# One program for the rotary projections and the attention loop, and a new order of the first expert group

## The reference, cut to what matters

```python
def _attn(x, ln_w, ln_b, conv_w, attn_w, proj_w, n_head):   # C = 256, n_head = 16, D = 16, T = 64
    h = _layernorm(x, ln_w, ln_b)
    hc = jax.lax.conv_general_dilated(pad(transpose(h)), conv_w, ...)     # 3 taps, per feature
    qkv = transpose(hc) @ attn_w
    q, k, v = jnp.split(qkv, 3, axis=-1)                                  # each (B, T, n_head, D)
    q = q * cos + _rotate_half(q) * sin
    k = k * cos + _rotate_half(k) * sin
    scores = jnp.einsum('bqhd,bkhd->bhqk', q, k) / jnp.sqrt(jnp.float32(D))
    p = jax.nn.softmax(jnp.where(causal, scores, -1e30), axis=-1)
    y = jnp.einsum('bhqk,bkhd->bqhd', p, v).reshape(B, T, C)
    return y @ proj_w
# x = x + _attn(...); then logits = layernorm(x) @ router_w, an argmax over four experts, and the chosen expert's FFN
```

## Time and profile before

| what | us |
|---|---|
| median of three runs | 2086.64 |
| lowest and highest run | 2083.78, 2087.58 |
| the profiled execution | 2082.32 |
| its span, first to last instruction | 2080.5 |
| TensorE busy | 1919.6 (92%) |
| VectorE busy | 1431.5 (69%) |
| ScalarE busy | 1103.8 (53%) |
| GpSimd busy | 848.8 (41%) |

### The profile page before, as it was taken

One profiled execution on the slowest core, in us unless ns is written; L12 is line 12 of the kernel. 1 busy time (PEld: TensorE's weight loads), 2 busy tenths in 40 slices (PEclk: granted clock), 3 DMA queues, 4 the chain that ended last, 5 costly groups with the idle time before them and its releaser, 6 DMA issues. The chain is left out here.

```text
span 2080.5 us, 35356 instructions
## 1 busy us (share of the span) xinstructions
PE 1919.6 (92%) x12240; PEld 1616.1 (78%) x12240; DVE 1431.5 (69%) x2403; ACT 1103.8 (53%) x2116; POOL 848.8 (41%) x855
## 2 busy tenths in 40 slices
PE   8999999999999999999998576999999666949998
PEld 6788888888888888888887455888899455839998
DVE  7767676767767676767776895432698565847776
ACT  5554555545555554555544697232455364636664
POOL 6350321405042240404200285130498144868885
PEclk9999999999999999999999699999999887969999
DMA  4101010010101010010102201310266114556661
GB/s 154 62 1 61 1 61 0 20 41 0 60 0 60 0 39 22 0 60 0 28 1 72 51 3 56 110 49 1 73 217 194 44 44 140 178 197 203 217 212 47
DMA packets 96322, 144.51 MB, mean 69 GB/s; under 512 B 15358, under 2 KB 72608, under 8 KB 96096
## 3 DMA queue, kind: packets, MB, share of 16 engines
q1 hardware_dynamic: 89168, 127.21, 19.0%
q0 software_dynamic: 4928, 12.86, 1.7%
q10 hardware_dynamic: 2128, 3.15, 0.4%
HBM read 111.46 MB, written 14.16 MB: 60 GB/s over the span
## 5 line engine op out<-in xcount | busy, mean ns | idle before, releaser
L317 PE MATMUL ps<-cond_x_lo,cond_w_hi 128*128 128x512 f32 x1008 | 393.4, 390 | 0.0
L468 ACT ACTIVATE cond_h_hi<-cond_h 128x512 fp32r<-128x512 f32 x288 | 174.0, 630 | 294.3 <-DVE cond_h L647 294.2
L781 POOL TENSOR_TENSOR cond_w_lo<-cond_stage_up,cond_w_hi 128x512 fp32r<-128x512 f32 x36 | 46.9, 1304 | 588.6 <-ACT cond_w_hi L468 588.6
L317 PE MATMUL ps<-cond_x_hi_first,cond_w_hi 128*128 128x512 f32 x578 | 230.8, 399 | 6.1 <-DVE cond_h L647 4.7
L378 PE MATMUL ps<-cond_h_hi,cond_d_hi 128*128 128x512 f32 x576 | 224.6, 390 | 2.6 <-DVE cond_h_lo L652 2.6
L317 PE MATMUL ps<-cond_x_hi_first,cond_w_lo 128*128 128x512 f32 x578 | 225.6, 390 | 0.0
L378 PE MATMUL ps<-cond_h_hi,cond_d_lo 128*128 128x512 f32 x576 | 224.2, 389 | 0.0
L378 PE MATMUL ps<-cond_h_lo,cond_d_hi 128*128 128x512 f32 x576 | 224.2, 389 | 0.0
L317 PEld LDWEIGHTS ps<-cond_x_lo,cond_w_hi 128*128 128x128 f32 x1008 | 189.9, 188 | 37.2
L630 DVE TENSOR_TENSOR ps<-cond_p_row,ps 128x512 f32<-128x512 f32 x142 | 98.6, 694 | 171.2 <-PE ps L317 171.1
L515 ACT ACTIVATE cond_h<-ps 128x512 f32<-128x512 f32 x216 | 124.6, 596 | 165.3 <-DVE cond_h_lo L652 132.1
(11 more groups left out here) (422 smaller groups left out, 5121.2 us busy)
## 6 DMA issues: line engine op xcount, KB each, us to landing
moe_stage_up<-in_L_ffn_expert_wv SPq DMA_DIRECT2D x22, 1024.0 KB, 9.2
typed_stage_up<-in_L_cond_wi SPq DMA_DIRECT2D x11, 1024.0 KB, 5.0
typed_stage_dn<-in_L_cond_wo SPq DMA_DIRECT2D x11, 1024.0 KB
moe_stage_dn<-in_L_ffn_expert_proj SPq DMA_DIRECT2D x11, 1024.0 KB
cond_stage_up<-in_L_cond_Wg SPq DMA_DIRECT2D x7, 1024.0 KB, 5.0
cond_stage_up<-in_L_cond_Wu SPq DMA_DIRECT2D x7, 1024.0 KB, 7.2
cond_stage_dn<-in_L_cond_Wd SPq DMA_DIRECT2D x7, 1024.0 KB, 9.4
rope_v_now<-rope_v_blk SPq DMA_DIRECT2D x16, 272.0 KB, 2.4
```

What stands on the lines that cost most here:

```text
L317: ins = pe.matmul(bank, ws[:, j, u, w], xs.rearrange("p o n -> p (o n)"), start=(opens and k == 0), stop=(k == 2), skip_group_check=True)
L468: copy = lambda dst, src: act.activation(dst, src, ACT.Copy)
L781: return pool.tensor_tensor(w_lo[:, j, :, A11:A12 + 1], raw_up[:, :, :, upper(j)], w_hi[:, j, :, A11:A12 + 1], ALU.subtract)
```

## The change

It has three parts. All three only move work or place it elsewhere in memory; what is computed is the same.

1. In the first stage, group 0: VectorE makes the hidden products as soon as their products are there, between the splits of T3 and T4; GpSimd splits T1 and T2 (new semaphore `x_lo_first`); ScalarE keeps both raw blocks of tokens (four copies instead of two). The split of the sums of chunk 0, which group 1 doesn't use, goes behind that of chunk 2, and `up_ready` is counted accordingly. ScalarE rounds hidden tiles of group 0 and then the weights of chunk 2 inside group 1.
2. `attention` becomes `hyper_attention` (the hyperbolic one, its lines unchanged) and `rotary`. The latter has one block: iterations 0 to 2 of the loop are written out between the projections 10 to 15, the loop's lists start at iteration 3 (EARLY). Projections use banks 4 to 7, since the loop's first phases use 0 to 3. The buffers u and prob lie where xT was, k_blk, x, qT and y in the space of s0, the projections' input, and pT in that of src_hi. So `bring(0)` waits for `src_ready` of all four wide tiles, `p_turn(0)` for the last `qk_taken` and `mix(0)` for the last `v_taken`. The router's weights are loaded at the beginning of the block. Four of the eight value copies follow in iterations 3 to 6, and the rotation of tile 15 in iteration 3.
3. At the end: VectorE does norm, weigh and lift of tile 15 (`finish`), GpSimd only its total. The logits of tiles 11 to 15 go to columns of their own in the bank (`late_ps`) and are copied together.

The diff, cut to its core:

```diff
@@ paired_experts
-                        pe.wait_ge(up_ready, J * e + j + 1)
+                        pe.wait_ge(up_ready, g if isinstance(g, int) and g <= 2 else J * e + j + 1)
...
+                def plain():                                   # VectorE
+                    plain_copy(0)
+                    hidden(0, 0, p2_done, bank_a, 0)
+                    split_t(T3)
+                    hidden(0, 0, p3_done, bank_d, 1)
+                    split_t(T4)
+                    plain_copy(1)
+                    dve.wait_ge(c22_made, 2)
+                    hidden(0, 0, c22_made, p5_row[:], 2)
+                    dve.wait_ge(x_lo_first, 2)
+                    dve.wait_ge(x_lo_dve, 6)
+                    split(0, 0, 12, 1)
+                    split(0, 0, 22, 2)
+                    hidden(0, 0, p4_done, bank_b[1], 3)
...
-                            plain_copy(0)
-                            for i in (T1, T2, T3, T4):
-                                split_t(i)
-                            dve.wait_ge(x_lo_dve, 8)
-                            dve.wait_ge(turned, 2 * TT)
-                            for t in range(2):
-                                keep_raw(1, t)
...
-                split_sums(0, 0)
-                split_sums(0, 1)
+                for n in range(2):                             # GpSimd
+                    pool.wait_ge(x_rounded, 2 * KC + n + 1)
+                    pool.tensor_tensor(x_lo[:, T1 + n:T1 + n + 1, cols(0)], t_first[:, n:n + 1], x_hi(T1 + n, 1, cols(0)),
+                                       ALU.subtract).then_inc(x_lo_first, 1)
+                split_sums(0, 1, 1)
                 split_down(0, 0)
+                raws(0, 2)
                 split_down(0, 1)
-                raws(0, 2)
-                split_sums(0, 2)
+                split_sums(0, 2, 2)
+                split_sums(0, 0, 3)
@@ rotary
+        u, prob = placed(m.xT_at, ("u", [2, H, T]), ("prob", [2, H, T]))
+        k_blk, x, qT, y = placed(src_at, ("k_blk", [2, KC, 2, GH, T]), ("x", [2, QK]), ("qT", [2, KC, P]), ("y", [2, D]))
+        pT, = placed(hi_at, ("pT", [2, HP, P]))
...
+                router.load(sp)                                # SyncE
+                double(0)
+                double(1)
+                sp.wait_ge(src_ready, TT)
+                bring(0, 0, 0)
+                bring(1, 1, 0)
+                double(2)
+                bring(2, 0, 1)
+                sp.wait_ge(ones_set, 1)
+                fetch(0, 0, 0)
+                double(3)
+                run(sp, "sync", ...)
...
+                for i in range(NP):                            # TensorE
+                    project(i)
+                    if i == 10:
+                        turn(0, 0, 0)
+                    elif i == 11:
+                        score(0, 0, 0)
+                    elif i == 12:
+                        turn(1, 1, 0)
+                    elif i == 14:
+                        score(1, 1, 0)
...
+                for i in range(NP):                            # ScalarE
+                    take_projections(i)
+                    if i == 3:
+                        round_src(2)
+                    elif i == 7:
+                        round_src(3)
+                        block_values(0, 0)
+                    elif i == 8:
+                        block_values(0, 1)
+                    elif i == 9:
+                        block_values(1, 0)
+                    elif i == 10:
+                        block_values(1, 1)
+                        take_q(0, 0, 0)
+                    elif i == 12:
+                        take_q(1, 1, 0)
+                    elif i == 14:
+                        exponential(0, 0, 0)
...
+                for i in range(NP):                            # VectorE
+                    times_cos(i)
+                    if i >= 1:
+                        rotate(i - 1)
+                    if i == 3:
+                        split_src(2)
+                    elif i == 7:
+                        split_src(3)
+                    elif i == 10:
+                        block_k(0, 0, 0)
+                    elif i == 12:
+                        clamp(0, 0, 0)
+                        top(0, 0, 0)
+                    elif i == 13:
+                        block_k(1, 1, 0)
...
+                for i in range(NP):                            # GpSimd
+                    times_sin(i)
+                    if i == 13:
+                        shift(0, 0, 0)
...
+                def finish(i, q, nth):                         # VectorE, in iteration i + 5, tile 15 alone
+                    dve.wait_ge(averaged, i + 1)
+                    dve.wait_ge(rstd_done, i + 1)
+                    dve.wait_ge(lifted, i - 1)
+                    dve.tensor_scalar(xn, router.x2[:, q], router.mean[:, q, 0:1], router.rstd[:, q:q + 1],
+                                      ALU.subtract, ALU.mult).then_inc(last_steps, 1)
+                    dve.wait_ge(last_steps, 1)
+                    dve.tensor_tensor(xn, xn, router.w[:], ALU.mult).then_inc(last_steps, 1)
+                    dve.wait_ge(last_steps, 2)
+                    dve.wait_ge(h_turned, i - 1)
+                    dve.wait_ge(stored[q], 16 * nth)
+                    dve.tensor_tensor(router.rows[:, q, 0:D], xn, router.b[:], ALU.add).then_inc(last_lifted, 1)
...
+                    wait(pe, kept, LATE if late(i) else i)     # route
+                    lg = late_ps[:, (i - LATE) * E_MOE:(i - LATE + 1) * E_MOE] if late(i) else lg_ps
```

More of the change, by code:

```diff
@@ L1 @@
+import math
 from contextlib import ExitStack
@@ L742, in expert @@
                             take(of_e, of_p, RIGHT if j == 0 else LEFT, first)
[L743 to L744 removed]
+                        combine(e, c, 1)
                         hidden(e, c, p2_done, bank_a, 0)
                         hidden(e, c, p3_done, bank_d, 1)
[L747 to L750 removed]
+                        lower_right(e, c, 1)
                         dve.wait_ge(c22_made, 2 * (CY * e + c) + 2)
@@ L1575, in hyper_units, with hyper_attention @@
     sem.give_back()
-def attention(nc, m, tag, hyper, srcT, resT, w, router=None, stored=None):
-    QK, GH = 2 * D, H // 4
+def hyper_attention(nc, m, tag, srcT, resT, w):
+    QK = 2 * D
     HP = H // 2
@@ L1660, in _ @@
                             n = 0
-                            more = hyper and cols.start == QK
+                            more = cols.start == QK
                             for k in range(KC):
@@ L1863, in _ @@
                             split_src(i // SUB + 2)
-                    later(NP - 1)
-                    if hyper:
-                        for part in range(6):
-                            norms(1, part)
-                        spikes()
+                    space_norm(NP - 1)
+                    for part in range(6):
+                        norms(1, part)
+                    spikes()
                 @block.gpsimd
@@ L1888, in _ @@
-                    if not hyper:
-                        for i in range(NP):
-                            times_sin(i)
-        sem.give_back()
-        if hyper:
-            hyper_units(nc, m, tag, resT, qk, v_blk, space, spike, wo, bo)
-            return
-        if hyper:
-            lag = dict(turn=0, q_blk=0, k_blk=0, score=0, clamp=1, root_sq=1, root_ln=2, root=2, root_add=2, dist_ln=2,
-                       dist=3, mask=3, top=3, shift=3, prob=4, p_turn=4, p_take=4, mix=5, y=5, y_turn=5, y_take=6,
-                       out=6, add=6, stretch=0, fetch=3)
-            order = dict(tensor="mix out turn p_turn y_turn score",
-                         scalar="y_take dist root_ln prob root q_blk root_sq p_take dist_ln",
-                         vector="stretch clamp y add k_blk top", gpsimd="mask root_add shift", sync="fetch")
-        else:
-            lag = dict(bring=0, turn=1, q_blk=1, k_blk=1, score=1, clamp=2, top=2, shift=2, prob=2, p_turn=3, p_take=3,
-                       mix=3, y=3, y_turn=4, y_take=4, out=4, fetch=2, bring_sum=3, bring_x=5, x2=4, stats=5, aggr=5, rstd=5,
-                       total=5, norm=5, weigh=5, lift=5, h_turn=8, h_take=8, route=9, keep=9, store=7)
-            order = dict(tensor="h_turn y_turn p_turn turn out mix route score",
-                         scalar="y_take h_take p_take rstd q_blk x2 prob",
-                         vector="stats clamp top aggr k_blk y keep", gpsimd="shift total norm weigh lift",
-                         sync="bring fetch bring_sum bring_x store")
@@ L1912, in attention @@
-        last = max(lag.values())
-        sem = StageSemaphores(nc, tag)
-        stretched, turned, k_turned, q_taken, k_blocked = (
-            sem(n) for n in ("stretched", "turned", "k_turned", "q_taken", "k_blocked"))
-        scored, clamped, root_squared, root_logged, rooted = (
-            sem(n) for n in ("scored", "clamped", "root_squared", "root_logged", "rooted"))
```

(3 more changed lines are left out.)

933 lines of the change are left out of this document (498 added, 435 removed).

## The result

| what | us |
|---|---|
| median before, beside it | 2085.72 (2083.78 to 2087.58) |
| median after | 2068.09 (2066.73 to 2071.58) |
| ratio | 0.9918, interval 0.9905 to 0.9930 |
| profiled execution, its span | 2071.58, 2069.8 (before: 2082.32, 2080.5) |
| measured again, beside the first experiments | 2070.38, ratio 0.9929 (0.9916 to 0.9943) |

What follows compares the result with a forecast made beforehand. The prediction took waits at the start, the join of rotary projections to attention loop, and the loop's end as the bounds; 3.5 + 14.5 + 2.4 = 20.4 us off the median 2086.64 gives 2066.2, range 2060.5 to 2076.

Steps and rivals of the forecast that it cites:

- Place 1, the start: First expert group: hidden products ahead of the T splits bring the first down product earlier; 3.5 us, bounds 1.5 and 5.5.
- what follows is as late relative to it as before: Start, behind the first down product: combine at 33.3, a wait of 0.8, so the 4.0 us lead is kept.
- Place 2, the join: Rotary projections to attention loop: the chain woven into the last projections gains 14.5 us, bounds 9 and 16.5.
- the brought tile's wait: Join, behind tile 10: TensorE waits 1.2 us, up to 2.4, for bring(0), with projection 11 and all others behind it.
- the wait for `k_blk(1)`: Join, score 1 behind projection 14: TensorE waits 1.8 us for VectorE's k_blk of tile 1, projection 15 behind it.
- covered: Join, tiles 7 to 10: ScalarE falls 1.2 us behind with four value copies; the banks and TensorE's wait absorb it.
- no wait for the brought tile, copies hidden: Join: the case behind the upper bound of its gain, 16.5 us.
- Place 3, the end: Loop's end: VectorE does norm, weigh and lift of tile 15, choose comes earlier; 2.4 us, bounds 1.5 and 3.5.
- The late bring: Rival at the join: bring lands 5 us late, score 1 as well; join gives 8, about 2073.5; chance 0.20.
- The clock falls at the join: Rival, TensorE's waits from 1728 to 1735: half clock lengthens the chain by 2.4 us, 2068.6; no chance of its own.
- The lead given back in the loop: Rival: the join's lead only makes tiles wait in the loop; places 1 and 3 remain, 5.9 us, 2080.7; chance 0.04.
- the stretch of the loop's operations by their place in memory: Rival: clamp, max and k_blk take 1.65 each instead of 1.2; 23 us over 17 iterations, 2089; chance 0.03.

Runs made afterwards that it cites:

- the first experiments: Before with the new start alone, 2081.88 us; before with the merged rotary block alone, 2074.62; after with the old end of the loop, 2073.66.
- the three kernels: After with value copies of tiles 4 to 7 moved later, 2071.62 us; with loads of x ahead of the second doubling, 2071.57; with both, 2066.37.
- the first kernels: Before with the merged rotary block alone, 2074.62 us; after with the old end of the loop, 2073.66 us.
- bring first: After with the loads of x of tiles 0 and 1 issued ahead of SyncE's second doubling: 2071.57 us, ratio 0.9937.

## Why the prediction was right, and where it wasn't
- **Place 1, the start: right in the first step, wrong in the second, and near the figure since two errors met.** The first product's wait fell from 4.68 to 0.23 us and is released by GpSimd's split of the sums, as said. The first down product started at 30.30 (29.5 to 30.0 in the other profiles; forecast 31.4), which is 1.1 to 1.9 better than forecast. The step that failed is "what follows is as late relative to it as before": it holds only if VectorE's operations keep their length, and they didn't, since the change also fills the 8 us in which GpSimd had been idle beside them. 5.1 became 2.4 here, and 5.5 to 5.9 became 2.7 to 3.6 in the others, against 3.5 forecast and bounds of 1.5 and 5.5. The postponed sum split, which the forecast guarded with 2 us, cost nothing that I could find.
- **Place 2, the join: 8.6 by this pair of traces, 7.4 of it at mix(1), instead of 14.5, under the lower bound of 9.** The places of both waits were right. Mis-sized were three terms: the brought tile's wait, 2.4 instead of 1.2; the wait for `k_blk(1)`, 2.9 instead of 1.8, because the add of tile 12 was stretched to 2.08; and the clock, which the forecast let fall behind 1728 only, for 2.4 us as a rival. It fell behind both waits, while projections followed, and cost 1.7 in projection 11, 0.9 in score(1) and 2.1 in projection 15. These are 1.2 + 1.1 + 4.7 = 7.0 of the 7.5 us by which the last projection was late. The 1.2 us between mix(1) and the last mix weren't won by the change: only the first profile of before is that long there. That ScalarE's value copies are "covered" was true only because of the wait at turn(0): it was the second cause behind the first, as the three kernels show, and with both removed the join gives 14.3. That is the forecast's figure, but not its case: for "no wait for the brought tile, copies hidden" the forecast had 16.5.
- **Place 3, the end: right.** 2.7 and 2.8 us, forecast 2.4. The three operations took 0.70, 0.90 and 0.83, so all were longer than the 0.42 estimated, and yet choose came no later than forecast, so what follows them was shorter than reckoned. Only the second and third have two tiles in SBUF as inputs, not all three as the prediction says. The Trainium skill ("SBUF — State Buffer", SBUF: two separate sides) has the second and third wait for a GpSimd operation, and the lift of tile 14 for them. The trace agrees for those two: each ended 0.3 us behind the GpSimd operation beside it (1832.19, where lift(14) ended at 1831.90; 1833.05, where the total of tile 15 ended at 1832.77). It doesn't for lift(14), which took its usual 0.72.
- **The sum.** Three places gave 2.4 + 8.6 + 2.7 = 13.7 in the traces, 6.7 less than the forecast, and 12.5 with the join's 7.4. The time came within 1.9 us of it (4.2 in the second measurement) only since the medians hold a gain that the traces don't. That was luck. Two small sums are off without effect: by its own terms the banks let 1.5 us pass, not 1.3, and the chances of "faster than 2082.5" hold 0.01 of the given-back lead, not most of its 0.04.
- **The rivals.** The late bring, at 2073.5, describes the join best (8 us, against 7.4 to 8.6 measured), though by other numbers: it was late by 2.4, not 5, and the clock did the rest. "The clock falls at the join" was the right mechanism, with its place 13 us too late and its price half. The lead given back in the loop is refuted: mix(1) and mix(3) are both 7.4 ahead and the stretch from mix(1) to the last mix is no longer than before. So is the stretch of the loop's operations by their place in memory: clamp, max and `k_blk` take 1.22, 1.22 and 1.20 on average, as in the earlier trace rows.

## What to carry to other kernels
Price a new wait between matmuls with what follows it: 2.4 us of waiting cost 4.1, because the next projection ran at half clock. When a step waits for one thing, look for what else would hold it a moment later; taking either away alone gained nothing in the time, both together did. When one stretch is compared in two traces, look how long it takes in other profiles before giving its tenths a cause. And before filling an engine's idle time, ask whose neighbour it is: waking GpSimd, or moving VectorE's work beside it, changes the length of VectorE's operations.

## What the runs showed of the hardware
- The same VectorE operation, two inputs in SBUF, 128x512, took 0.68 us with GpSimd silent, 1.22 to 1.60 beside GpSimd operations of 0.7 to 1.7 us, and 1.56 to 2.92 beside its splits of 128x512 and 128x1024 (1.7 to 2.4). The Trainium skill ("SBUF — State Buffer", Who interferes with whom) says that the later of the two is blocked until the earlier one is done, whole instruction by whole instruction; the trace agrees, in that the loss grows with the length of the neighbour's instruction.
- A wait of 2.3 to 2.6 us at turn(0) was followed by some 3 us at half clock in all six profiles that have it (after and the first kernels, those with the values or `k_blk(1)` moved). The second wait, at score(1), was so in the four profiles with after's join (2.85 or 2.86 in three of them, 3.34 in the kernel with the join alone): score(1) took 1.99. Where the earlier wait lay elsewhere or was gone, score(1) took 1.09 behind 2.85, 2.86 and 3.06 of waiting, and projection 15 then ran at full clock twice and fell in its course once (bring first). The length of the wait alone doesn't decide.
- Of the two profiled executions of before, both were faster than nearly all of its timed ones (2082.32 and 2080.71 against a median of 2085.7), so a difference between two traces can be several microseconds off the difference between medians.
